# Moving one batch's gates, factors and projections ahead of the others, with the other batches' projections between its first queries and scores

## The chip, the cores and the metric

The kernel runs on one core of one Trainium2 chip. The core has a matrix engine (TensorE, PE in the rows), a vector engine (VectorE, DVE), an activation engine (ScalarE, ACT), a general engine (GpSimd, POOL) and a queue engine for transfers (SyncE, SP). Each works through its own list of instructions in order; semaphores join the lists. The time is that of one execution on the device, in microseconds.

## What is computed

One decoder layer over x of 4 batches x 512 tokens x 256 features: a layernorm, attention with 16 heads of 128, a layernorm and a residual; then a layernorm, a mixture of 8 experts (2 chosen for each token) plus a shared network, a layernorm and a residual. The attention is the part that matters here:

```python
q = (x @ Wq.T).reshape(b, n, H, D)
kv = x @ Wkv.T
kv_head = x @ Wkvh.T
g = x @ Wg.T
log_f = jnp.concatenate([jnp.zeros((b, 1, 2 * H), jnp.float32), jax.nn.log_sigmoid(g)], axis=1)
log_f_cumsum = jnp.cumsum(log_f, axis=1)[:, :-1]
kv_head = kv_head * jnp.exp(log_f_cumsum)
kv_head = jnp.cumsum(kv_head, axis=1)
kp, vp = (kv[..., :D], kv[..., D:])
kh, vh = (kv_head[..., :H], kv_head[..., H:])
k = jnp.einsum('bnd,bnh->bnhd', kp, kh)
v = jnp.einsum('bnd,bnh->bnhd', vp, vh)
q = rope(q)
k = rope(k)
```

Keys and values are shared by all heads but for a factor for each head and token. That factor is a running sum of a projection, weighted by a running product of sigmoids (the gates). Scores are masked to the past, a softmax and the weighing of values follow, and a projection out.

## The kernel before, in words

The order of the work is written out by hand, one list for each engine. A unit is one head of one batch; there are 64, batch by batch. Matrix products that must be as exact as float32 are made of three passes over operands that are split into a high and a low part (`three_pass`, L377): ACT or POOL rounds the high part, DVE or POOL subtracts to get the low one. Transposes (L765, L855) and the weighing of values (L869) are plain float32.

The front works on all four batches before the first unit. For each batch, DVE takes the statistics of x (L1102, L1105), ACT the root (L514), DVE the reciprocal and the normalized x (L1109, L1116). PE turns it (`turn_x`, L765), ACT and DVE split it (`head_of`, `rest_of`: xt_hi L521, xt_lo L1123). PE then projects gates, keys and values from w0, which POOL has split (w_hi L1530, w_lo L1532; the rows drop the number in a name). Keys are swapped on ACT (L534, L535), multiplied by cosines on DVE (L1130) and by sines on POOL (L1545), and summed on DVE into kt (L1136). When the gates of all batches are copied, ACT takes one sigmoid over 128 rows (L569) and DVE computes the factors of all batches at once (`factors`: scan L1146, product L1148, scan L1149). SP stores them in DRAM and loads each unit's key factors back as a row spread over 128 partitions (kh_row). PE turns them into columns (L931) that scale the turned probabilities (vcol, L647).

Queries of a unit (L377) are swapped on ACT (L577, L578), rotated on DVE and POOL (L1176, L1560, L1565), and split by ACT (q_hi L611) and POOL (q_lo L1569). Keys of a unit are scaled on POOL (L1574) and split by ACT (k_hi L605) and DVE (k_lo L1203). Then follow scores on PE (L837), maxima on DVE (L1184), exponentials on ACT (L589), turned probabilities on PE (L855), whose eviction scales them (ACT L598, DVE L1197), weighing of values (L869), division by the sums (DVE L1211), a split of the output (ACT L617, POOL L1579) and its projection (L885). Queries run four units ahead, scores two. In units 1 to 8, DVE also takes the rest of a later head's wq (`rest_of_wq`, L1223), in units 1 to 14 the rest of a head's wo (L1228).

## Time and profile before

| what | us |
|---|---|
| runs of the kernel | 839.72, 846.82, 848.85 (median 846.82) |
| the profiled execution | 842.17 |
| its span in the trace | 840.40 |
| what lies around the span | 1.77 |
| busy: PE, DVE, POOL, ACT | 760.9, 614.5, 553.7, 490.4 |

The span is what the trace covers. The rows give, for an instruction, its start from the span's start and its length; an engine's idle time before it and what ended that stand in brackets.

### The profile page before, as it was taken

Reading aid. Unit: us, or ns where it says so; the run is one execution under the profiler, and the core shown is the slowest. Engines: PE = TensorE matmul, PEld = TensorE weight load, DVE = VectorE, ACT = ScalarE, POOL = GpSimd, SP = SyncE. Lnnn points to the kernel's source line nnn. Section 1 sums busy time; section 2 is a strip of 40 time slices with the busy share of each in tenths; the row PEclk is TensorE's granted clock in tenths of the full one; section 3 lists DMA queues with packets and bytes.
Section 4 is the critical chain, followed back from the end, with each engine's and each line's share of the span. In section 5 each row is a group of like instructions: output and inputs, shape, how many; then the busy total and the mean of one; then the engine's idle time right before and its main releaser. Section 6 shows DMA issues by size and latency. Waiting matters only on the chain.

```text
...
## 1 busy us (share of the span) xinstructions
PE 760.9 (91%) x4344; PEld 634.0 (75%) x4344; DVE 614.5 (73%) x1561; ACT 490.4 (58%) x1155; POOL 553.7 (66%) x460
## 2 busy tenths in 40 slices
...
GB/s 305 50 88 58 69 83 151 136 136 64 64 76 62 66 70 63 72 64 64 77 64 64 76 63 64 72 43 26 128 82 72 110 144 186 186 76 94 100 88 51
DMA packets 47701, 75.74 MB, mean 90 GB/s; under 512 B 9680, under 2 KB 24592, under 8 KB 47632
## 3 DMA queue, kind: packets, MB, share of 16 engines
...
q8 instruction: 34, 0.56, 0.3%
q14 instruction: 35, 0.29, 0.1%
...
## 4 chain that ended last, share of the span: by engine, by line
PE 75%; DVE 9%; ACT 5%; issue 5%; another core or an unknown queue 3%; POOL 2%; DMA 1%; DVEq 0%; ACTq 0%; POOLq 0%
PE ps L377 19%; PE ps L869 17%; PE ps L837 14%; PE ps L885 11%; PE ps L855 8%; PE ps L980 5%; DVE xn L1116 1%; DVE hid_both L1468 1%; DMA x_sb<-in_x_dram 1%; DVE hid_hi L1458 1%; DVE hid L1463 1%; DVE hid L1455 1%; DVE s_hid L1396 1%; ACT y_sb L750 1%
## 5 line engine op out<-in xcount | busy, mean ns | idle before, releaser
L589 ACT ACTIVATE prob<-ps,neg_max 128x512 f32<-128x512 f32 (+3 forms) x256 | 132.6, 526 | 86.2 <-DVE neg_max L1184 86.2
L869 PE MATMUL ps<-pt,vp 128*128 128x512 f32 (+3 forms) x512 | 150.7, 437 | 4.6 <-issue 3.1
L869 PEld LDWEIGHTS ps<-pt,vp 128*128 128x128 f32 x512 | 83.2, 192 | 54.6 <-issue 19.1
L1569 POOL TENSOR_TENSOR q_lo<-q_sw,q_hi 128x512 fp32r<-128x512 f32 x64 | 85.9, 1342 | 47.9 <-ACT q_hi L611 47.9
L1184 DVE CUSTOM_DVE_ANT_0 ps<-ps,causal_row 128x512 f32<-128x512 f32 (+3 forms) x256 | 117.4, 520 | 0.0
L1579 POOL TENSOR_TENSOR o_lo<-o_t,o_hi 128x512 fp32r<-128x512 f32 x64 | 83.3, 1301 | 47.3 <-ACT o_hi L617 46.8
L837 PE MATMUL ps<-k_hi,q_hi 128*128 128x512 f32 (+3 forms) x256 | 91.0, 355 | 7.3 <-POOL q_lo L1569 5.0
L855 PE MATMUL ps<-id_f,prob 128*128 128x128 f32 x640 | 92.3, 275 | 2.4 <-ACT pt L598 2.4
L1203 DVE TENSOR_TENSOR k_lo<-kh_row,k_hi 128x512 fp32r<-128x512 f32 x64 | 83.4, 1303 | 8.1 <-ACT k_hi L605 8.1
L1560 POOL TENSOR_TENSOR q_sw<-q_sw,rope_sb 128x512 f32<-128x512 f32 x64 | 83.7, 1307 | 8.7 <-ACT q_sw L578 8.7
L1565 POOL TENSOR_TENSOR q_sw<-q_cos,q_sw 128x512 f32<-128x512 f32 x64 | 81.5, 1274 | 9.2
L1574 POOL TENSOR_TENSOR kh_row<-kt,kh_row 128x512 f32<-128x512 f32 x64 | 85.5, 1336 | 0.0
L1197 DVE TENSOR_SCALAR pt<-ps,vcol 128x384 f32<-128x384 f32 (+2 forms) x192 | 82.1, 476 | 2.9 <-PE ps L855 2.8
L837 PE MATMUL ps<-k_hi,q_lo 128*128 128x512 f32 (+3 forms) x256 | 83.9, 328 | 0.0
L837 PE MATMUL ps<-k_lo,q_hi 128*128 128x512 f32 (+3 forms) x256 | 83.8, 327 | 0.0
L1176 DVE TENSOR_TENSOR q_cos<-ps,rope_sb 128x512 f32<-128x512 f32 x64 | 44.2, 690 | 53.0 <-ACT q_sw L578 52.7
L855 PEld LDWEIGHTS ps<-id_f,prob 128*128 128x128 f32 x640 | 72.5, 140 | 11.2 <-issue 2.9
L980 PE MATMUL ps<-sdn_sb,s_hid 128*128 128x256 f32 (+1 forms) x192 | 55.8, 437 | 19.0 <-DVEq L1376 16.2
L577 ACT COPY q_sw<-ps 64x512 f32<-64x512 f32 x64 | 37.3, 582 | 51.4 <-PE ps L377 48.9
L980 PEld LDWEIGHTS ps<-sdn_sb,s_hid 128*128 128x128 f32 (+1 forms) x192 | 37.5, 210 | 35.8 <-ACT y_sb L691 16.8
L1396 DVE TENSOR_TENSOR s_hid<-s_sg,ps 128x512 f32<-128x512 f32 (+1 forms) x24 | 16.1, 686 | 63.8 <-PE ps L377 22.6
L377 PE MATMUL ps<-xt_hi,wq_hi 128*128 128x512 f32 x128 | 52.7, 412 | 7.1 <-DVE q_cos L1130 6.2
...
## 6 DMA issues: line engine op xcount, KB each, us to landing
kh_row<-kvh_rows SPq DMA_DIRECT2D x64, 256.0 KB, 3.2
inv_row<-inverse_sums SPq DMA_DIRECT2D x64, 256.0 KB, 3.1
...
```

The costliest lines, as they stand in the source:

```text
L377: last = pe.matmul(psum, w(o), m(o), start=(o == 0 and j == 0), stop=(o == EO - 1 and j == 2))
L589: ins = act.activation(prob[:, i % 2, ROW_AT[nt]:ROW_AT[nt] + w], ps_s[bank][:, at:at + w], ACT.Exp, scale=-1.0, bias=neg_max[:, i % 2, nt ...
L837: ins = pe.matmul(ps_s[bank][:, at:at + w], q_[:, r, qs], k_[:, r, 0:w], start=(nt == tiles[0] and j == 0), stop=(nt == tiles[-1] and j == 2))
L855: ins = pe.transpose(ps_pt[bank][:, dst:dst + P], prob[:, i % 2, src:src + P], id_f[:])
L869: ins = pe.matmul(ps_qo[:, mt * P:SEQ], vp[:, b * TPB + mt, :], pt[:, i % 2, cols], start=(mt == 0), stop=(mt == PT_BANKS[-1][-1]))
L885: ins = pe.matmul(ps_acc[t // 2][:, at:at + E], o_[:, r, t * P:(t + 1) * P], w[:, h, :], start=(h == 0 and j == 0 and t % 2 == 0), stop=(h ...
L980: ins = pe.matmul(ps[6 + half][:, q * E:(q + 1) * E], s_hid[0:SHW[n][i], j % 2, i, t * P:(t + 1) * P], sdn_sb[0:SHW[n][i], n, i, :], start ...
L1184: ins = dve.tensor_tensor_reduce(s_, s_, causal_row[:, (NT - 1 - nt) * P:], 1.0, BIG, ALU.add, ALU.min, neg_max[:, i % 2, nt:nt + 1])
L1203: dve.tensor_tensor(k_lo[:, i % 2, :], kh_row[:, i % 2, :], k_hi[:, i % 2, :].bitcast(F32), ALU.subtract) \
L1560: pool.tensor_tensor(q_sw[:], q_sw[:], sin_sb, ALU.mult).then_inc(q_sin_ready, 1)
L1569: pool.tensor_tensor(q_lo[:, i % 2, :], q_sw[:], q_hi[:, i % 2, :].bitcast(F32), ALU.subtract) \
L1574: pool.tensor_tensor(kh_row[:, i % 2, :], kt[:, tok(batch(i))], kh_row[:, i % 2, :], ALU.mult) \
```

## The change

Batch 0 goes first and alone through gates, factors and projections, so that its factors can be stored while the others' projections have yet to be made. Those of batches 1 to 3 stand on PE between the first queries and scores. The factors are computed twice: for batch 0 (32 rows) in the front, and for all batches (128 rows) on DVE in units 0 to 3, stored in unit 4, turned on PE in unit 5. The sigmoid is now an exponential on ACT and an add and a reciprocal on DVE. Units 0 and 1 use plain float32 queries and keys (`PLAIN = 2`), with no split; their keys are scaled on DVE. Keys of a batch are summed on POOL instead of DVE. The root, the reciprocal and the normalizing of x for batches 1 to 3 go to POOL and ACT. The split of w0 goes to ACT and, after x of batch 0 is normalized, POOL. The rest of wq for heads 8 to 15 goes from DVE to POOL, in units 1 to 8. x of batch 0 is loaded in two halves, from two queues; the cosines and sines come after it. The diff, cut to its core:

```diff
+        FACTOR_STEP = 5
...
+        PLAIN = 2
+        q_rot = place("q_rot", Y_AT + 8 * KB, [PLAIN, SEQ])
+        kh = place("kh", Y_AT + 12 * KB, [PLAIN, SEQ])
...
-            sp.dma_start(x_sb[:, 0:TPB, :], x_v[0]).then_inc(x_in[0], 16)
+            sp.dma_start(x_sb[:, 0:2, :], x_v[0, :, 0:2, :]).then_inc(x_in[0], 16)
+            sp.dma_start(w0_raw[:], w0).then_inc(w0_in, 16)
             sp.dma_start(id_f[:], ident).then_inc(id_in, 16)
-            sp.dma_start(w0_raw[:], w0).then_inc(w0_in, 16)
...
-            sp.dma_start(kvh_dram, hc_t).then_inc(kvh_stored, 16)
+            sp.dma_start(kvh_dram[0:2 * H, :], hc_t[0:2 * H, :]).then_inc(kvh_stored, 16)
...
-            load_shared(0)
...
+                if i == FACTOR_STEP - 1:
+                    sp.wait_ge(hc_ready, 2)
+                    sp.dma_start(kvh_dram[2 * H:, :], hc_t[2 * H:, :]).then_inc(kvh_stored, 16)
+                if i == FACTOR_STEP:
+                    sp.wait_ge(kvh_stored, 32)
+                    load_shared(0)
...
+            act.dma_start(x_sb[:, 2:TPB, :], x_v[0, :, 2:TPB, :]).then_inc(x_in_rest, 16)
...
+                act.activation(f_t[rows, :], src[2 * H:4 * H, :], ACT.Exp, scale=-1.0).then_inc(gate_copied, 1)
...
+                if i == FACTOR_STEP:
+                    factors_as_columns(1)
                 if wq_head(i) is not None:
...
+            def turn_factors(k):
+                pe.wait_ge(hc_ready, k + 1)
+                bank, n = (5, 2 * H * B) if k else (3, 2 * H)
+                for mt in range(TPB):
+                    ins = pe.transpose(ps[bank][:, mt * n:(mt + 1) * n], hc_t[0:n, mt * P:(mt + 1) * P], id_f[0:n, 0:n])
+                ins.then_inc(vcol_psum, 1)
...
-                        for j, (q_, k_) in enumerate(((q_hi, k_hi), (q_hi, k_lo), (q_lo, k_hi))):
+                        passes = ((q_rot, kh),) if i < PLAIN else ((q_hi, k_hi), (q_hi, k_lo), (q_lo, k_hi))
+                        for j, (q_, k_) in enumerate(passes):
...
+            turn_x(0)
+            gates(0)
+            keys(0)
+            values(0)
+            turn_x(1)
             queries(0)
+            gates(1)
+            keys(1)
+            values(1)
             queries(1)
+            turn_x(2)
+            turn_factors(0)
+            pe.wait_ge(k_cos_ready, 1)
             pe.wait_ge(vcol_ready, 1)
             scores(0)
             queries(2)
+            gates(2)
+            keys(2)
+            values(2)
+            turn_x(3)
             scores(1)
+            gates(3)
+            keys(3)
             queries(3)
+            values(3)
             pe.wait_ge(v_ready, B)
             for i in range(UNITS):
...
                 weigh_values(i)
+                if i == FACTOR_STEP:
+                    turn_factors(1)
...
+            def sigmoids(k):
+                n = 2 * H * B if k else 2 * H
+                dve.wait_ge(gate_copied, B if k else 1)
+                done(dve.tensor_scalar(f_t[0:n, :], f_t[0:n, :], 1.0, None, ALU.add))
+                done(dve.reciprocal(f_t[0:n, :], f_t[0:n, :]))
...
-                if i and wq_head(i - 1) is not None:
-                    rest_of_wq(wq_head(i - 1))
+                if i == 0:
+                    sigmoids(1)
+                if i == 1:
+                    products_of_gates(1)
+                if i == 2:
+                    scaled_gates(1)
+                if i == 3:
+                    sums_of_gates(1)
...
             pool.wait_ge(w0_hi_ready, 1)
+            pool.wait_ge(xn_ready, TPB)
             pool.tensor_tensor(w0_lo[:], w0_raw[:], w0_hi[:].bitcast(F32), ALU.subtract).then_inc(w0_split, 1)
...
                 if i + 3 < UNITS:
                     rest_of_queries(i + 3)
+                if i and wq_head(i - 1) is not None:
+                    rest_of_wq(wq_head(i - 1), wq_head(i - 1) + 1)
```

On DVE in the front, before the change, the factors of all batches (128 rows) stand behind the keys of three batches:

```order
L1130 SCALAR_TENSOR_TENSOR q_cos<-ps,rope_sb 128x512 [waits k_swapped,kt_ready]
L1123 TENSOR_TENSOR xt_lo<-ps,xt_hi 128x512 [waits xt_hi_ready] x2
L1136 TENSOR_TENSOR kt<-q_cos,q_sw 128x512 [waits k_sin_ready,k_cos_ready]
L1130 SCALAR_TENSOR_TENSOR q_cos<-ps,rope_sb 128x512 [waits k_swapped,kt_ready]
L1136 TENSOR_TENSOR kt<-q_cos,q_sw 128x512 [waits k_sin_ready,k_cos_ready]
L1144 MEMSET fcum_t 128x1
L1146 SCALAR_TENSOR_TENSOR fcum_t<-f_t,ones_t 128x511 [waits f_ready]
L1148 TENSOR_TENSOR kvh_t<-kvh_t,fcum_t 128x512 [waits dve_c]
L1149 SCALAR_TENSOR_TENSOR hc_t<-ones_t,kvh_t 128x512 [waits dve_c]
L1130 SCALAR_TENSOR_TENSOR q_cos<-ps,rope_sb 128x512 [waits k_swapped,kt_ready]
L1136 TENSOR_TENSOR kt<-q_cos,q_sw 128x512 [waits k_sin_ready,k_cos_ready]
```

After it, batch 0's factors (32 rows: add, reciprocal, scan, product, scan; a scan is listed as SCALAR_TENSOR_TENSOR) stand ahead of the rest of x of batch 1 (xt_lo):

```order
L1185 TENSOR_SCALAR f_t<-f_t 32x512 [waits gate_copied]
L1186 RECIPROCAL f_t<-f_t 32x512 [waits dve_c]
L1190 MEMSET fcum_t 32x1 [waits dve_c]
L1191 SCALAR_TENSOR_TENSOR fcum_t<-f_t,ones_t 32x511
L1177 SCALAR_TENSOR_TENSOR k_cos<-ps,rope_sb 128x512 [waits k_swapped,rope_in,dve_c]
L1196 TENSOR_TENSOR kvh_t<-ps,fcum_t 32x512
L1203 SCALAR_TENSOR_TENSOR hc_t<-ones_t,kvh_t 32x512 [waits dve_c]
L1170 TENSOR_TENSOR xt_lo<-ps,xt_hi 128x512 [waits xt_hi_ready] x2
L1207 TENSOR_TENSOR q_cos<-ps,rope_sb 128x512 [waits q_swapped]
```

The factors moved from behind the keys to a place ahead of the second batch's split, and two instructions of a new kind joined them.

On ACT ahead of the first unit, before the change, the second unit's exponentials (L589) follow the third unit's query swap and splits, and a copy of values (vp) is long past:

```order
L577 COPY q_sw<-ps 64x512 [waits q_ready,q_psum]
L578 COPY q_sw<-ps 64x512
L605 CAST k_hi<-kh_row 128x512 [waits s_psum,kh_scaled]
L611 CAST q_hi<-q_sw 128x512 [waits s_psum,q_sum_ready]
L589 ACTIVATE prob,row_sum<-ps,neg_max 128x512 [waits max_ready]
L589 ACTIVATE prob,row_sum<-ps,neg_max 128x384 [waits max_ready]
L589 ACTIVATE prob,row_sum<-ps,neg_max 128x128
L589 ACTIVATE prob,row_sum<-ps,neg_max 128x256 [waits max_ready]
L548 CAST wo_hi<-wo_raw 128x256 [waits wo_in0] x2
```

After it, the gates, keys and values of the last batch (kvh_t, f_t, k_sw, vp) stand directly ahead of them:

```order
L552 COPY kvh_t<-ps 32x512 [waits gate_psum]
L553 ACTIVATE f_t<-ps 32x512
L560 ACTIVATE k_sw<-ps 64x512 [waits kt_ready,k_psum]
L561 ACTIVATE k_sw<-ps 64x512
L565 COPY vp<-ps 128x512 [waits v_psum]
L592 ACTIVATE prob,row_sum<-ps,neg_max 128x512 [waits max_ready]
L592 ACTIVATE prob,row_sum<-ps,neg_max 128x384 [waits max_ready]
L592 ACTIVATE prob,row_sum<-ps,neg_max 128x128
L592 ACTIVATE prob,row_sum<-ps,neg_max 128x256 [waits max_ready]
L574 CAST wo_hi<-wo_raw 128x256 [waits wo_in0] x2
```

The exponentials of the second unit now wait for the last batch's values on PE.

On DVE at the start of unit 0, before the change, from the rest of wo to the eviction of turned probabilities (pt):

```order
L1228 TENSOR_TENSOR wo_lo<-wo_raw,wo_hi 128x256 [waits wo_hi_ready,vcol_ready]
L1228 TENSOR_TENSOR wo_lo<-wo_raw,wo_hi 128x256 [waits wo_hi_ready]
L1217 RECIPROCAL row_inv<-row_sum 128x4 [waits exp_ready]
L1218 STREAM_TRANSPOSE inv_t<-row_inv 128x128 [waits dve_c]
L1176 TENSOR_TENSOR q_cos<-ps,rope_sb 128x512 [waits q_swapped]
L1197 TENSOR_SCALAR pt<-ps,vcol 128x384 [waits pt_psum]
L1197 TENSOR_SCALAR pt<-ps,vcol 128x128
L1197 TENSOR_SCALAR pt<-ps,vcol 128x256 [waits pt_psum]
```

After it:

```order
L1254 TENSOR_TENSOR wo_lo<-wo_raw,wo_hi 128x256 [waits wo_hi_ready,vcol_ready]
L1254 TENSOR_TENSOR wo_lo<-wo_raw,wo_hi 128x256 [waits wo_hi_ready]
L1248 RECIPROCAL row_inv<-row_sum 128x4 [waits exp_ready]
L1249 STREAM_TRANSPOSE inv_t<-row_inv 128x128 [waits dve_c]
L1185 TENSOR_SCALAR f_t<-f_t 128x512 [waits gate_copied]
L1186 RECIPROCAL f_t<-f_t 128x512 [waits dve_c]
L1207 TENSOR_TENSOR q_cos<-ps,rope_sb 128x512 [waits q_swapped,dve_c]
L1228 TENSOR_SCALAR pt<-ps,vcol 128x384 [waits pt_psum]
L1228 TENSOR_SCALAR pt<-ps,vcol 128x128
L1228 TENSOR_SCALAR pt<-ps,vcol 128x256 [waits pt_psum]
```

An add and a reciprocal over 128 rows and 512 columns came between the inverses of the sums and the cosine.

## Rows read from the trace of the kernel before

**Rows 1.** Engine busy time in stretches: us, busy us (x instructions) by engine, clock, DMA, GB/s

```profile
42.00:62.00 20.00, 11.97 (x54) 10.34 (x55) 7.13 (x8) 6.41 (x11) 9.49 (x8) 0.70 0.29 92
...
80.90:150.40 69.50, 66.04 (x382) 54.45 (x383) 69.23 (x146) 49.50 (x127) 53.25 (x41) 1.00 0.31 99
```

**Rows 2.** The chain that ended last, its start: start us, us, what

```profile
0.73 5.26 DMA x_sb<-in_x_dram
...
8.49 3.16 DVE xn L1116 x4
...
15.21 2.91 PE ps L377 x6
...
21.36 1.38 DVE xn L1116 x4
...
28.40 1.09 PE ps L765 x8
...
29.50 6.81 PE ps L377 x42
...
49.47 0.58 ACT q_sw L577
```

**Rows 3.** Timeline of the front: start us, us, engine, line, instruction, idle before it

```profile
8.14 0.82 POOL L1530 CAST w_hi<-w_raw 128x768 fp32r<-128x768 f32 x1 [7.09 <-DMA w_raw<-in_w_dram]
...
38.84 2.38 POOL L1537 TENSOR_TENSOR wq_lo<-wq_raw,wq_hi 128x1024 fp32r<-128x1024 f32 x1
...
38.99 2.79 DVE L1136 TENSOR_TENSOR kt<-q_cos,q_sw 128x512 f32<-128x512 f32 x1 [0.67 <-POOL q_sw L1545]
...
41.70 1.21 DVE L1146 TENSOR_TENSOR_SCAN fcum_t<-f_t,ones_t 128x511 f32<-128x511 f32 x1
...
42.95 0.69 DVE L1148 TENSOR_TENSOR kvh_t<-kvh_t,fcum_t 128x512 f32<-128x512 f32 x1
...
57.83 0.77 PE L837 MATMUL ps<-k_hi,q_hi 128*128 128x512 f32 x1 [3.50 <-POOL q_lo L1569]
...
77.12 1.26 DVE L1197 TENSOR_SCALAR pt<-ps,vcol 128x384 f32<-128x384 f32 x3
```

**Rows 4.** DMA issues of the first 80 us: count, KB each, median us to landing

```profile
rope_sb<-in_cos_t_dram ACTq DMA_DIRECT2D x1, 256.0 KB, 4.4
```

**Rows 5.** Groups of DVE instructions by shape: busy us, mean ns

```profile
L1217 DVE RECIPROCAL row_inv<-row_sum 128x4 f32<-128x4 f32 x64 | 10.8, 169 | 4.2 <-ACT prob L589 4.2
...
L1435 DVE RECIPROCAL cw<-den 128x16 f32<-128x16 f32 x1 | 0.3, 253 | 0.0
```

**Rows 6.** Stretches of the front, as in rows 1; the clock follows PEclk's place after POOL

```profile
9.00:11.70 2.70, 0.00 (x0) 0.00 (x0) 2.70 (x5) 0.00 (x0) 1.80 (x1) 1.00 1.11 349
...
46.50:49.90 3.40, 3.37 (x10) 2.71 (x11) 0.66 (x1) 0.43 (x1) 0.00 (x0) 0.50 0.32 120
...
57.80:63.60 5.80, 5.77 (x17) 5.05 (x18) 0.69 (x1) 1.74 (x4) 3.78 (x3) 0.50 0.08 25
```

**Rows 7.** Timeline of one unit between 99.6 and 108.4 us

```profile
99.75 1.29 POOL L1579 TENSOR_TENSOR o_lo<-o_t,o_hi 128x512 fp32r<-128x512 f32 x1 [0.60 <-ACT o_hi L617]
...
100.06 1.25 DVE L1223 TENSOR_TENSOR wq_lo<-wq_raw,wq_hi 128x256 fp32r<-128x256 f32 x1
...
101.00 1.46 POOL L1574 TENSOR_TENSOR kh_row<-kt,kh_row 128x512 f32<-128x512 f32 x1
...
103.45 2.40 PE L869 MATMUL ps<-pt,vp 128*128 128x512 f32 x8 [0.41 <-issue]
...
105.22 0.69 ACT L589 ACTIVATE prob<-ps,neg_max 128x512 f32<-128x512 f32 x1 [1.80 <-DVE neg_max L1184]
```

**Rows 8.** Page, costliest groups: busy us, mean ns, idle before

```profile
L589 ACT ACTIVATE prob<-ps,neg_max 128x512 f32<-128x512 f32 (+3 forms) x256 | 132.6, 526 | 86.2 <-DVE neg_max L1184 86.2
```

**Rows 9.** Timeline of POOL in units 10 and 11

```profile
166.13 1.79 POOL L1569 TENSOR_TENSOR q_lo<-q_sw,q_hi 128x512 fp32r<-128x512 f32 x1 [0.73 <-ACT q_hi L611]
...
174.08 1.79 POOL L1569 TENSOR_TENSOR q_lo<-q_sw,q_hi 128x512 fp32r<-128x512 f32 x1 [0.73 <-ACT q_hi L611]
```

More of the change, by code:

```diff
@@ L235, in decoder_layer @@
         neg_half = small("neg_half", [TPB])
+        neg_mean = small("neg_mean", [TILES])
         neg_max, row_sum = (small(n, [2, NT]) for n in ("neg_max", "row_sum"))
@@ L847, in turn_probs @@
                         pe.wait_ge(pt_rest_ready, 2 * i - 1)
+                    if k == 1 and i == FACTOR_STEP + 1:
+                        pe.wait_ge(vcol_ready, 2)
                     if k == 2:
@@ new lines, in scaled_gates, with sums_of_gates @@
+            def scaled_gates(k):
+                n = 2 * H * B if k else 2 * H
+                done(dve.tensor_tensor(kvh_t[0:n, :], kvh_t[0:n, :] if k else ps[GATE_BANK[0]][0:n, :], fcum_t[0:n, :], ALU.mult))
+            def sums_of_gates(k):
+                n = 2 * H * B if k else 2 * H
+                if k:
+                    dve.wait_ge(vcol_ready, 1)
+                    dve.wait_ge(kvh_stored, 16)
+                dve.tensor_tensor_scan(hc_t[0:n, :], ones_t[0:n, :], kvh_t[0:n, :], 0.0, ALU.mult, ALU.add).then_inc(hc_ready, 1)
```

349 lines of the change are left out of this document (175 added, 174 removed).

## Prediction

> **What bounds the kernel now.** I read the time by stage first [rows 1]. From 80.9 to 150.4 us, which is eight of the 64 attention units (1 to 8), VectorE (DVE) is busy 69.23 of 69.50 us: it sets a pace of 8.7 us a unit, and TensorE (PE) follows. From 42 to 62 us PE is busy 11.97 of 20 us and no engine more than that: a stretch of waits. So the change, which rearranges what lies ahead of the first units, can gain there, and whatever it hands DVE or POOL in units 0 to 8 costs time.
>
> The chain that ended last then shows what the front is made of [rows 2]. x of batch 0 takes 5.26 us to land; normalizing it takes DVE 3.16 us where the same four instructions take 1.38 us for batch 2; the first projection starts at 15.21. The 42 matmuls from 29.50 on (gates, values, gates, keys) take 6.81 us. The timeline of the late front [rows 3] has the gates' scan at 41.70, PE idle for 3.50 us before the first scores at 57.83, and at 77.12 DVE's first eviction of turned probabilities, my **marker**: from there on DVE has no rest.
>
> The same rows show a rule for DVE and POOL. At 38.99 DVE's sum of two SBUF tiles takes 2.79 us: it ends 0.56 us after POOL's 2.38 us split that began at 38.84. One waits until the other is through. The slow 3.16 us of [rows 2] lie beside POOL's split of w0, which begins at 8.14.
>
> **The change, part by part.** I follow the clock of the profiled execution (842.17 us, span 840.40) to the marker, then count the units.
>
> *To the first gates.* x of batch 0 now comes as two halves of 256 KB, first on two queues. The nearest row is the cosine table, 256 KB and first on ACT's queue, issued at 0.74: 4.4 us, so 5.14 [rows 4] instead of 5.99: 0.85 us gained. The split of w0 now waits until x is normalized: 3.16 becomes 1.38, 1.78 us gained. Against that, x of batch 1 is 1216 KB deep in SP's queue and DVE reads its statistics before the rest of batch 0. w0, 960 KB deep in the old order, was there at 8.14 [rows 3]; 256 KB more at 349 GB/s [rows 6] make 0.7 us alone and twice that if ACT's queue takes its share, so 8.9 to 9.6, where DVE would be free at 9.0. I take 0.6 us lost, bounds 0 and 1. The first gates start at 15.21 - 0.85 - 1.78 + 0.6 = 13.2.
>
> *The gates' factors.* Six matmuls at the low clock take 2.91 us [rows 2], the exponential on ACT 0.6 as its other 512-column copies (the one at 49.47): 16.7. Then DVE works in order: add one, reciprocal over 512 columns, scan, cosine of the keys, product, second scan, and only then the rest of x of batch 1, for which the second gates wait. Add, cosine, product and each of the two rests I take at 0.69 us, as the product at 42.95, and a scan at 1.21 [rows 3]. The reciprocal is the unknown. Its rows [rows 5] give 169 ns for 4 columns and 253 ns for 16: 7 ns a column, so 0.169 + 508 x 0.007 = 3.7 us. If the slope is an accident of small tiles, it is as long as another 512-column instruction, 0.6 us. I take 3.7, since a slope between rows of the same instruction is the nearest evidence, and keep 0.6 for the range.
>
> With 0.6 us for the second scan's wait behind POOL's sum of the keys, DVE takes 0.6 + 3.7 + 1.2 + 0.7 + 0.7 + 0.6 + 1.2 + 1.4 = 10.1 us: the second gates start at 26.8. PE has nothing to do from about 23: its keys, values and first queries are 36 matmuls, 5.8 us by the rate of [rows 2], with the turn of batch 1 7 us behind the first gates' end at 16.1.
>
> *To the first scores.* Gates, keys and values of batch 1 and one head's queries are the same 42 matmuls: 6.81 us. After idle stretches of 6.1 and 3.5 us, PE ran at a granted clock of 0.50 (1.2 of 2.4 GHz) for 3.4 and 5.8 us [rows 6]; after an idle 3.8 us I add 2.5 us. The turn of batch 2 (1.09 at the high clock [rows 2]) stands before the first scores on PE, and on ACT its heads stand before the swap of the second queries and the copy of the factors: 0.6 + 1.2 + 0.4 us. The factors' bank holds the first scores back: 26.8 + 6.8 + 2.5 + 1.1 + 2.2 = 39.4, against 57.83 [rows 3].
>
> *To the marker.* That head start of 18 us is not kept. Between the first scores and unit 0 now lie the blocks of batches 2 and 3 with two queries (2 x 6.81), a turn (1.09) and two scores. A plain score has the shapes of a unit's weighing of values, 2.40 us [rows 7], and I charge that; what plain scores take away are the splits of keys and queries on ACT, POOL and DVE, which no longer stand in this path. Together 19.5 us: values of batch 3 end at 58.9. The second unit's exponentials now stand behind the copy of these values on ACT. So: copy 0.6, exponentials 4 x 0.526 [rows 8], two splits of wo 0.8, DVE's rest of wo 0.4, inverses 0.5, then the new add and second reciprocal 0.6 + 3.7, 0.1 between them, and the cosine 0.7: 9.5 us. The marker falls at 68.4 instead of 77.12: **8.7 us gained**.
>
> *Units 1 to 3.* DVE's rest of wq goes, scans and a product come. In before's unit the rest of wq is 1.25 us long, but until 101.04 it waits for POOL's o_lo, so only 0.27 of it is work [rows 7]; a scan of 1.21 in its place ends 0.94 later, POOL's kh_row waits behind it and DVE's rest of wo behind that. About 1.0 each for the two scans, 0.4 for the product. POOL's new rest of wq costs some 0.75 us (2.38 for 1024 columns and 1.29 for 512, carried on to 256) ahead of o_lo in units 2 and 3: 0.3 each. Lost: 3.0 us; bounds 0 and 5.
>
> *Units 4 to 8.* DVE is relieved, but POOL is not free: in a later unit, 7.95 us from q_lo to q_lo, its only idle time is the 0.73 us in which it waits for q_hi [rows 9]. With 0.75 more it comes to 8.7, what DVE needed before; 0.5 of q_lo's 1.79 is a wait for DVE that may go. Gained 0 to 2.5, I take 0.5.
>
> *Unit 5.* The factors of the other batches are turned on PE after that unit's weighing, and ACT stops for them before its exponentials. In before's unit the weighing ends at 105.85, the exponentials start at 105.22 [rows 7]; with the turn, the copy and a split of wq they start some 2 us later, and q_hi, q_lo and the next scores with them. Lost: 2.0; bounds 0.5 and 2.5.
>
> Later loads, the deferred load of the shared weights and everything from unit 9 on are alike. **Sum:** -8.7 + 3.0 - 0.5 + 2.0 = -4.2 us, 842.17 becomes 838.0. The median of the runs, 846.82, lies 4.65 above the profiled execution; I forecast it at 838.0 + 4.6 = 842.6. About 1% is what a measurement of this kernel can tell from no change.
>
> **The rivals.** *The reciprocal is as fast as other instructions.* Then the front and unit 0 each lose 3.1 us: 842.6 - 6.2 = 836.4, faster by 1.2%. For it: only two short tiles show the slope. Against: it is the same instruction and 84 ns for twelve columns are no noise.
>
> *The units swallow the new work.* POOL's gaps and the vanished wait of q_lo hide the rest of wq, ACT catches up after unit 5: the 5.0 us of units 1 to 5 fall away, 837.6. For it: ACT is busy 49.50 of 69.50 us there and POOL 53.25 [rows 1]. Against: DVE is full, and its waits are chained to POOL's.
>
> *PE stays at the low clock.* From 39.4 to 58.9 PE has queries, blocks, turns and scores with a wait before many of them; if two thirds of this run at 0.50, as did 57.8 to 63.6 [rows 6], the 19.5 us grow by 13: 855.6, slower. It decides from some 4 us of it on. Against: 6.81 us for 42 matmuls at 29.50 came in a stretch as dense as this one.
>
> **How the numbers follow.** Forecast 0.52; fast reciprocal 0.16 and swallowed work 0.20, together faster by over 1% with 0.36; low clock 0.12, slower by over 1%; within 1% 0.52. The range, 831 to 853, goes from the fast reciprocal with all of the swallowed work (836.4 - 5.0) to the forecast with eight of the low clock's 13 us and the upper bounds of units 1 to 5 (2.5 more). The forecast's own range is 838.5 to 849.
>
> **What would show it.** Right: the first gates near 13 us, a reciprocal of 32x512 near 3.7, PE idle some 4 us before the second gates, the first scores near 39, the second unit's exponentials directly behind the last copy of values, the marker near 68, unit 1 above 9 us, a gap before the exponentials of unit 7. Wrong: a marker before 65 or after 72, units 1 to 3 at 8.7 us or less, or units 4 to 8 at 8.0.

## The result, and the profile after

| | before | changed | changed, measured again |
|---|---|---|---|
| median of the runs, us | 843.35 (12 runs) | 833.94 (12 runs) | 835.23 (4 runs; before beside it: 842.98) |
| ratio to before, 95% interval | | 0.9876, 0.9857 to 0.9895 | 0.9899, 0.9884 to 0.9914 |
| span of the profiled execution | 840.40 | 833.2 | 834.1 |
| first gates | 15.21 | 13.49 | 13.81 |
| second gates | | 27.19 | 27.51 |
| first scores | 57.83 | 37.35 | 39.14 |
| marker: first eviction of turned probabilities | 77.12 | 64.90 | 66.67 |
| turned row sums of unit 12 | 167.67 | 156.59 | 158.32 |
| from there to the end of the span | 672.7 | 676.6 | 675.8 |

The change makes the kernel faster by 1.0 to 1.2%, 8 to 10 us. That is inside the range (831 to 853), but below the forecast's own range (838.5 to 849): faster by over 1%, which had 0.36, came, and not the likeliest case. Of the 8.7 us between the forecast (842.6) and the median, 3.5 are the starting point, since the three runs of the kernel before that it stood on have a median of 846.82 and all twelve one of 843.35. The other 5.2 are the change: 4.2 us forecast, 9.4 measured. The last row of the table is scatter: over the fourteen profiled executions of this study, which all run the same work there, it lies between 672.2 and 676.6. The two executions of the changed kernel happen to have its highest values; from unit 12 to unit 63 they are within 0.5 us of the kernel before, and the difference lies behind that. So I compare executions at unit 12, and below that by the length of a stage.

The timeline of the changed kernel's first profiled execution (start us, us, engine, line, instruction, idle before it), in the order in which the prediction walked:

```profile
6.68 1.38 DVE L1163 TENSOR_SCALAR xn<-x_sb,mv,rstd 128x256 f32<-128x256 f32 x4
...
8.22 1.81 POOL L1586 TENSOR_TENSOR w_lo<-w_raw,w_hi 128x768 fp32r<-128x768 f32 x1 [7.17 <-DVE xn L1163]
...
10.06 1.40 DVE L1148 BATCH_NORM_STATS2 stats<-x_sb 128x6 f32<-128x256 f32 x4 [2.00 <-DMA x_sb<-in_x_dram]
...
12.07 1.28 DVE L1170 TENSOR_TENSOR xt_lo<-ps,xt_hi 128x512 fp32r<-128x512 f32 x2
...
13.49 0.77 PE L387 MATMUL ps<-xt_hi,w_hi 128*128 128x512 f32 x1 [3.34 <-DVE xt_lo L1170]
...
18.06 3.34 DVE L1186 RECIPROCAL f_t<-f_t 32x512 f32<-32x512 f32 x1
...
27.19 0.47 PE L387 MATMUL ps<-xt_hi,w_hi 128*128 128x512 f32 x1 [3.39 <-DVE xt_lo L1170]
...
37.35 2.40 PE L861 MATMUL ps<-kh,q_rot 128*128 128x512 f32 x8 [1.84 <-issue]
39.40 0.59 PE L387 MATMUL ps<-xt_hi,wq_hi 128*128 128x512 f32 x1
...
56.82 0.69 ACT L592 ACTIVATE prob<-ps,neg_max 128x512 f32<-128x512 f32 x1
...
59.37 0.76 DVE L1254 TENSOR_TENSOR wo_lo<-wo_raw,wo_hi 128x256 fp32r<-128x256 f32 x2 [5.03 <-ACT wo_hi L574]
...
60.91 3.35 DVE L1186 RECIPROCAL f_t<-f_t 128x512 f32<-128x512 f32 x1
...
64.90 1.26 DVE L1228 TENSOR_SCALAR pt<-ps,vcol 128x384 f32<-128x384 f32 x3
...
65.09 4.61 PE L896 MATMUL ps<-pt,vp 128*128 128x512 f32 x8 [2.69 <-issue]
```

They answer to [rows 2, 3]. Normalizing takes 1.38 us instead of 3.16, since POOL's split starts behind it. VectorE then waits 2.00 us for x of batch 1, and the rest of x of batch 0 stands behind those statistics. The reciprocal takes 3.34 us; TensorE waits 3.39 us for what VectorE does after it. First scores start 20.5 us earlier than before, the marker 12.2. The last rows are unit 0: VectorE idles 5.03 us, then runs a second reciprocal of 3.35 us for which everything waits, and TensorE, idle for 2.69 us, weighs at half speed (4.61 us; 2.40 in [rows 7]).

Stretches of the same execution, as in [rows 1] (us, busy us by engine, granted clock after POOL's column): unit 0's weighing, and units 1 to 8.

```profile
65.00:69.80 4.80, 4.61 (x8) 2.28 (x8) 3.04 (x12) 2.67 (x9) 2.53 (x2) 0.50 0.00 0
...
71.15:140.26 69.11, 66.89 (x394) 55.61 (x393) 57.53 (x140) 50.30 (x128) 60.28 (x48) 1.00 0.39 115
```

The granted clock of the weighing is 0.50, 1.2 of 2.4 GHz. VectorE, 69.23 of 69.50 us busy before, is now busy 57.53 of 69.11, and POOL 60.28 instead of 53.25. Units 1 to 9 last 9.55, 8.54, 9.03, 8.12, 9.46, 8.04, 8.35, 8.02, 8.35 us (from one turned row sums to the next), where before's first eight lasted 8.72 each and the ninth 7.58.

### The profile page after: what moved, and what is told of

The parts are those of the page before. It is cut to its first block, busy times and chain, and to the rows that moved or that the text cites. A ratio compares the mean times of both kernels' runs of the same rounds, so it can differ in the third digit from the quotient of the medians.

```text
span 833.2 us, 13978 instructions
## 1 busy us (share of the span) xinstructions
PE 756.6 (91%) x4340; PEld 629.5 (76%) x4340; DVE 598.4 (72%) x1548; ACT 492.8 (59%) x1159; POOL 562.6 (68%) x473
## 4 chain that ended last, share of the span: by engine, by line
PE 72%; DVE 7%; POOL 6%; issue 5%; ACT 5%; another core or an unknown queue 3%; DMA 1%; SPq 0%; DVEq 0%; ACTq 0%; POOLq 0%
PE ps L387 21%; PE ps L896 15%; PE ps L861 12%; PE ps L912 9%; PE ps L882 7%; PE ps L1023 6%; POOL o_lo L1643 1%; POOL q_lo L1633 1%; POOL kh_row L1638 1%; DMA x_sb<-in_x_dram 1%; POOL q_sw L1629 1%; POOL q_sw L1621 1%; DVE hid_both L1523 1%; ACT prob L592 1%
## 5 line engine op out<-in xcount | busy, mean ns | idle before, releaser
L1643 POOL TENSOR_TENSOR o_lo<-o_t,o_hi 128x512 fp32r<-128x512 f32 x64 | 85.2, 1332 | 43.3 <-ACT o_hi L620 43.3
L1633 POOL TENSOR_TENSOR q_lo<-q_sw,q_hi 128x512 fp32r<-128x512 f32 x62 | 83.5, 1347 | 42.3 <-ACT q_hi L614 42.3
L861 PE MATMUL ps<-k_hi,q_hi 128*128 128x512 f32 x248 | 87.1, 351 | 0.0
L1629 POOL TENSOR_TENSOR q_sw<-q_cos,q_sw 128x512 f32<-128x512 f32 x62 | 78.9, 1272 | 11.7 <-DVE q_cos L1207 2.9
L1638 POOL TENSOR_TENSOR kh_row<-kt,kh_row 128x512 f32<-128x512 f32 x62 | 83.5, 1346 | 0.0
L861 PE MATMUL ps<-k_lo,q_hi 128*128 128x512 f32 x248 | 80.3, 324 | 0.0
L861 PE MATMUL ps<-k_hi,q_lo 128*128 128x512 f32 x248 | 80.1, 323 | 0.0
L1207 DVE TENSOR_TENSOR q_cos<-ps,rope_sb 128x512 f32<-128x512 f32 x64 | 44.1, 688 | 49.6 <-ACT q_sw L581 49.2
L1234 DVE TENSOR_TENSOR k_lo<-kh_row,k_hi 128x512 fp32r<-128x512 f32 x62 | 74.1, 1196 | 0.0
L1242 DVE TENSOR_TENSOR o_t<-ps,inv_row 128x512 f32<-128x512 f32 x64 | 44.2, 691 | 15.1 <-PE ps L896 14.3
```

The lines of the kernel that those rows point to most:

```text
L861: ins = pe.matmul(ps_s[bank][:, at:at + w], q_[:, r, qs], k_[:, r, 0:w], start=(nt == tiles[0] and j == 0), stop=(nt == tiles[-1] and j == ...
L1629: pool.tensor_tensor(q_sw[:], q_cos[:], q_sw[:], ALU.add).then_inc(q_sum_ready, 1)
L1633: pool.tensor_tensor(q_lo[:, i % 2, :], q_sw[:], q_hi[:, i % 2, :].bitcast(F32), ALU.subtract) \
L1638: pool.tensor_tensor(kh_row[:, i % 2, :], kt[:, tok(batch(i))], kh_row[:, i % 2, :], ALU.mult) \
L1643: pool.tensor_tensor(o_lo[:, i % 2, :], o_t[:], o_hi[:, i % 2, :].bitcast(F32), ALU.subtract) \
```

## The experiments

Times and starts, for all of them (the ratio is to the kernel before, run beside each):

| run | median | ratio (95%) | first scores | marker | unit 12 |
|---|---|---|---|---|---|
| second reciprocal earlier | 829.49 | 0.9831 (0.9794 to 0.9868) | 40.07 | 64.12 | 154.75 |
| sigmoid of batch 0 on ScalarE | 831.54 | 0.9856 (0.9818 to 0.9893) | 34.42 | 61.96 | 154.30 |
| factors copied late | 832.69 | 0.9860 (0.9824 to 0.9896) | 40.28 | 69.50 | 160.11 |
| rest of wq back on VectorE | 839.00 | 0.9945 (0.9923 to 0.9967) | 40.03 | 67.58 | 164.51 |
| rest of x first | 832.15 | 0.9877 (0.9853 to 0.9901) | 38.29 | 65.84 | 157.46 |
| before, rest of wq on POOL | 839.74 | 0.9959 (0.9941 to 0.9977) | 59.17 | 78.48 | 165.30 |
| before, new loads | 841.25 | 0.9978 (0.9956 to 1.0001) | 56.92 | 76.23 | 166.81 |
| no plain units | 836.89 | 0.9929 (0.9905 to 0.9953) | 37.65 | 70.04 | 161.15 |
| the three combined | 824.18 | 0.9777 (0.9763 to 0.9790) | 35.26 | 60.98 | 150.57 |
| front in another order | 822.16 | 0.9743 (0.9728 to 0.9759) | 32.95 | 58.68 | 148.21 |
| split of w0 at once | 833.27 | 0.9885 (0.9869 to 0.9901) | 38.87 | 66.43 | 158.08 |

**The changed kernel again.** No edit.

> The changed kernel unaltered, a second profiled execution of it. Theory: TensorE's clock in the second gates differs from execution to execution, since three kernels with this same front showed 512-column matmuls of 0.77 us there and the first scores at 40.0 to 40.3 where the first profiled execution of the changed kernel had 0.47 and 37.35; so first scores at either 37.4 or 40.1, everything from unit 1 on in the same periods (9.55, 8.54, 9.03, 8.12, 9.46, 8.04, 8.35, 8.02). Rival, it is the edits that moved the clock: first scores at 37.4 again. Ratio 0.9876 by both.

Timeline and stretches of the second execution:

```profile
27.51 0.76 PE L387 MATMUL ps<-xt_hi,w_hi 128*128 128x512 f32 x1 [4.28 <-DVE xt_lo L1170]
...
39.14 2.40 PE L861 MATMUL ps<-kh,q_rot 128*128 128x512 f32 x8 [1.85 <-issue]
```

```profile
27.50:30.20 2.70, 2.69 (x6) 2.13 (x7) 2.40 (x11) 0.00 (x0) 1.44 (x2) 0.50 0.37 104
...
30.70:34.00 3.30, 3.30 (x26) 3.08 (x25) 0.67 (x2) 2.10 (x4) 3.13 (x8) 1.00 0.07 27
```

The clock differs, without any edit: 0.50 from 27.5 to 30.2 here, 1.00 in the first execution. From second gates to first scores it is 11.63 us, there 10.16. The three kernels that the expectation means (second reciprocal earlier, factors copied late, rest of wq back on VectorE) show 12.69, 12.99 and 12.71. So a front in which TensorE waits some 3 to 5 us (2.9 to 5.1) before the second gates came out with the low clock in six of eight executions and without it in two. That is part of why single runs differ by 3 us. The Trainium skill (TensorE: Matmul & The Clock Gate, What's actually happening) says that how many matmuls of one kernel run cold, at the low clock, differs from run to run; these traces agree, with 0 and 1.5 us in two executions of one kernel and 2.5 in others with the same front. The periods of units 1 to 8 are the same to 0.03 us.

**Second reciprocal earlier.**

```diff
             cos_of_keys(3)
+            sigmoids(1)
             dve.wait_ge(vcol_ready, 1)
...
-                if i == 0:
-                    sigmoids(1)
```

> The changed kernel with the add and the second reciprocal (128x512) taken out of unit 0 and put where VectorE waits 5.03 us for the head of wo, behind the cosine of batch 3's keys. Theory A, the chain ahead of the units goes 1:1 to the end: the marker (first eviction of turned probabilities) falls from 64.90 to 61.1, the turned row sums of unit 12 from 156.6 to 152.8, and to 150.5 if the weighing of unit 0 also runs at the high clock then (2.32 instead of 4.61 us); the median near 830, ratio to the kernel before 0.981 to 0.984. Theory B, the units' own pace decides and swallows a head start: the marker at 61.1 too, but unit 12 within 1 us of 156.6 and the ratio at 0.987.

The timeline of this kernel, VectorE and TensorE ahead of unit 0:

```profile
57.94 3.35 DVE L1186 RECIPROCAL f_t<-f_t 128x512 f32<-128x512 f32 x1
...
62.11 0.76 DVE L1254 TENSOR_TENSOR wo_lo<-wo_raw,wo_hi 128x256 fp32r<-128x256 f32 x2 [0.82 <-ACT wo_hi L574]
...
64.94 2.32 PE L896 MATMUL ps<-pt,vp 128*128 128x512 f32 x8
```

The reciprocal sits in the idle time, of which 0.82 us are left, and the weighing runs in 2.32 us. This execution had the slower second gates, so it is read from the first scores: 24.05 us to the marker instead of 27.55, and 114.68 to unit 12 instead of 119.24, 4.6 us less: 3.5 ahead of the marker, and 1.1 behind it, where the half-speed weighing stood. The median fell by 4.5 against 833.94, though the intervals of the two ratios overlap. Theory A holds, and the half-speed weighing was part of the reciprocal's price.

**Sigmoid of batch 0 on ScalarE.**

```diff
-                act.activation(f_t[rows, :], src[2 * H:4 * H, :], ACT.Exp, scale=-1.0).then_inc(gate_copied, 1)
+                if b:
+                    act.activation(f_t[rows, :], src[2 * H:4 * H, :], ACT.Exp, scale=-1.0).then_inc(gate_copied, 1)
+                else:
+                    act.activation(f_t[rows, :], src[2 * H:4 * H, :], ACT.Sigmoid).then_inc(gate_copied, 1)
+                    act.activation(std[:, 8:9], eps_sb[:, 0:1], ACT.Exp)
```

VectorE's add and reciprocal stay for the other batches (k = 1).

> The changed kernel with the sigmoid of batch 0 on ScalarE, as the kernel before has it, in place of exponential, add and first reciprocal (32x512); one small exponential behind it brings ScalarE's exponential table back. Theory A, VectorE's chain of the factors sets the front: 3.75 us fewer on it, the second gates start at 23.9 instead of 27.19 with nothing left of TensorE's 3.39 us of idle, first scores at 34 instead of 37.35, marker at 61.6, ratio 0.984. Rival: the transfers set it (the factors' way through DRAM and back, 27.53 to 32.1, or x of batch 2), then the second gates come at 24 but the first scores stay within 1 us of 37.35 and the ratio at 0.987.

The timeline of this kernel from ScalarE's sigmoid to the first scores:

```profile
15.69 1.28 ACT L556 ACT_TABLE_LOAD   x1
...
17.59 1.28 ACT L557 ACT_TABLE_LOAD   x1
...
17.61 1.21 DVE L1196 TENSOR_TENSOR_SCAN fcum_t<-f_t,ones_t 32x511 f32<-32x511 f32 x1 [1.63 <-issue]
...
24.28 0.47 PE L387 MATMUL ps<-xt_hi,w_hi 128*128 128x512 f32 x1 [1.23 <-DVE xt_lo L1174]
...
34.42 2.40 PE L865 MATMUL ps<-kh,q_rot 128*128 128x512 f32 x8 [1.85 <-issue]
```

The scan starts at 17.61, where the add stood. Both table loads (1.28 us each) are there, the second while ScalarE has nothing else to do. Second gates and first scores come 2.9 us earlier than in the first execution of the changed kernel, and TensorE stays at the high clock: theory A, but for 1.23 us of TensorE's wait that are left where it had none. Of the 2.9 us, 2.3 are left at unit 12, since unit 1 takes 10.15 us instead of 9.55; the median is 2.4 us lower.

**Factors copied late.**

```diff
-                if i == FACTOR_STEP:
-                    factors_as_columns(1)
                 if wq_head(i) is not None:
...
                     exps(i + 2, [1, 2])
+                if i == FACTOR_STEP:
+                    factors_as_columns(1)
```

> The changed kernel with the copy of the other batches' factors put behind unit 7's exponentials on ScalarE (in its list for unit 5), where it stood ahead of them. Theory: ScalarE's 2.10 us of waiting for the turned factors is what makes unit 5 take 9.46 us beside 8.0 to 8.4 of its neighbours: unit 5 falls to 8.2, unit 12 from 156.6 to 155.4, ratio 0.9860. Rival: TensorE's four turns and the wait in front of unit 6's second bank make the unit long, or the copy then holds the head of the output: unit 5 and 6 together stay within 0.3 us of 17.5, ratio 0.9876.

ScalarE's copy in the timeline of the changed kernel:

```profile
112.41 0.32 ACT L652 COPY vcol<-ps 128x192 f32<-128x192 f32 x1 [2.10 <-PE ps L832]
```

The same copy in this kernel, and the exponential it now follows:

```profile
118.36 0.47 ACT L592 ACTIVATE prob<-ps,neg_max 128x256 f32<-128x256 f32 x1
...
118.81 0.32 ACT L652 COPY vcol<-ps 128x192 f32<-128x192 f32 x1
```

The 2.10 us of waiting are gone; unit 5 takes 8.22 us instead of 9.46, unit 6 8.22 instead of 8.04. Marker to unit 12 is 90.61 instead of 91.69: 1.1 us, as the theory has it. The ratios alone would not tell it (the intervals overlap).

**Rest of wq back on VectorE, and before with it on POOL.** The same edit in both directions; in the kernel before:

```diff
-                if i and wq_head(i - 1) is not None:
-                    rest_of_wq(wq_head(i - 1))
...
                     rest_of_queries(i + 3)
+                if i and wq_head(i - 1) is not None:
+                    rest_of_wq(wq_head(i - 1), wq_head(i - 1) + 1)
```

The first of these two kernels takes POOL's lines out of the changed kernel's unit and gives VectorE its `rest_of_wq` back, ahead of the rest of wo.

> The changed kernel with the rest of wq for heads 8 to 15 back on VectorE, as before the change. By the prediction's terms: units 1 to 3 lose about 1 us each (VectorE has the rest of wq and the scans), units 4 to 8 go from 8.0 to 8.4 back to 8.7: unit 12 at 160 to 162, ratio 0.992 to 0.994. Rival, what POOL is rid of makes up for it: unit 12 within 1 us of 156.6, ratio 0.987 to 0.989.

> The kernel before with one part of the change alone: the rest of wq for heads 8 to 15 goes from VectorE to the end of POOL's unit. Theory A, the rest of wq is what holds VectorE at 8.72 us a unit: units 1 to 8 take 8.0 to 8.4, unit 9 some 0.8 longer, so the turned row sums of unit 12 come 2.5 to 4 us earlier than 167.67, counted from the marker, and the ratio is 0.995 to 0.997. Theory B, it is the way in which VectorE and POOL wait for each other (a rest of wq is 0.38 us of work and 1.25 with its wait): the unit stays at 8.5 to 8.8 with the wait elsewhere, ratio 0.999 to 1.002.

With it back on VectorE, units 1 to 8 take 10.18, 10.42, 10.84, 8.95, 9.95, 8.12, 8.13, 8.13: marker to unit 12 is 96.93 instead of 91.69, 5.2 us more, and the median 5.1 more. The sum is as expected (unit 12 at 161.8, if counted from the first scores of the changed kernel's first execution; the ratio is just above its range), its place is not: units 1 to 5 lose 5.6 us, up to 1.9 each, and units 6 to 8 take 8.1 us where 8.7 was expected. With it on POOL in the kernel before, units 1 to 8 take 65.25 us instead of 69.74 and unit 9 0.75 more: 3.7 us less from marker to unit 12, and a ratio of 0.9959. These are theory A's times, but the cause is theory B's. The timeline of VectorE and POOL in the kernel before, from the end of unit 6 into unit 7:

```profile
124.01 1.29 POOL L1569 TENSOR_TENSOR q_lo<-q_sw,q_hi 128x512 fp32r<-128x512 f32 x1 [1.29 <-ACT q_hi L611]
...
124.22 1.62 DVE L1203 TENSOR_TENSOR k_lo<-kh_row,k_hi 128x512 fp32r<-128x512 f32 x1
...
125.89 1.28 POOL L1579 TENSOR_TENSOR o_lo<-o_t,o_hi 128x512 fp32r<-128x512 f32 x1 [0.59 <-ACT o_hi L617]
...
126.21 1.25 DVE L1223 TENSOR_TENSOR wq_lo<-wq_raw,wq_hi 128x256 fp32r<-128x256 f32 x1
```

The same place in the kernel before with the rest of wq on POOL:

```profile
122.41 0.68 DVE L1203 TENSOR_TENSOR k_lo<-kh_row,k_hi 128x512 fp32r<-128x512 f32 x1
...
123.02 1.29 POOL L1567 TENSOR_TENSOR q_lo<-q_sw,q_hi 128x512 fp32r<-128x512 f32 x1 [0.73 <-ACT q_hi L611]
...
124.26 0.74 POOL L1535 TENSOR_TENSOR wq_lo<-wq_raw,wq_hi 128x256 fp32r<-128x256 f32 x1
...
124.35 0.18 DVE L1217 RECIPROCAL row_inv<-row_sum 128x4 f32<-128x4 f32 x1 [1.26 <-ACT prob L589]
...
124.95 1.29 POOL L1577 TENSOR_TENSOR o_lo<-o_t,o_hi 128x512 fp32r<-128x512 f32 x1
```

Before, VectorE's rest of the keys (k_lo) starts 0.2 us after POOL's q_lo and takes 1.62 us, then the rest of wq starts 0.3 us after POOL's o_lo and takes 1.25. Without the rest of wq, VectorE comes to k_lo before POOL comes to q_lo and does it in 0.68; it even waits 1.26 us for ScalarE. POOL has 0.74 us more to do and is not late, since its own waits for ScalarE (1.29 and 0.59 us above) shrink to 0.73 and nothing. The Trainium skill (SBUF — State Buffer, SBUF: two separate sides) calls this a lock held for a whole instruction, by whichever engine starts first; the first fence agrees with that, since k_lo and the rest of wq end 0.5 and 0.3 us behind the instruction of POOL that began before them. How much of the 1.25 us was work shows in the changed kernel with the rest of wq on VectorE, in a unit of 8.13 us, where VectorE comes first:

```profile
130.34 0.68 DVE L1234 TENSOR_TENSOR k_lo<-kh_row,k_hi 128x512 fp32r<-128x512 f32 x1
...
132.52 0.38 DVE L1254 TENSOR_TENSOR wq_lo<-wq_raw,wq_hi 128x256 fp32r<-128x256 f32 x1
...
132.62 1.43 POOL L1650 TENSOR_TENSOR o_lo<-o_t,o_hi 128x512 fp32r<-128x512 f32 x1 [0.44 <-ACT o_hi L620]
```

In units 6 to 8 of this kernel VectorE and POOL run the same instructions in the same order as in units 6 to 8 of the kernel before, in 8.13 us a unit instead of 8.72. So 8.72 us was not the amount of VectorE's work: it was one of two rhythms of the same work, the one in which VectorE comes second each time. Moving the rest of wq ended that rhythm; what else would end it was not tested.

**Before, with the new loads.** Loads as in the change, and in front of POOL's split of w0:

```diff
             pool.wait_ge(w0_in, 16)
+            pool.wait_ge(xn_ready, TPB)
             pool.tensor_copy(w0_hi[:], w0_raw[:]).then_inc(w0_hi_ready, 1)
```

> The kernel before with the change's order of loads and with POOL's split of w0 held back until x of batch 0 is normalized. By the prediction's terms the first gates come 0.9 + 1.8 - 0.6 = 2.1 us earlier, at 13.1 to 13.5 instead of 15.21. Theory A, the front is one chain: the first scores come as much earlier than 57.83, ratio 0.9975. Theory B, the later batches set the front (their x, VectorE's and POOL's work on the keys): the first scores move by under 0.5 us, ratio 1.000.

First gates at 13.34, 1.9 us earlier; first scores 0.9 earlier than in the kernel before, and 2.25 earlier than in the run with the rest of wq on POOL, which has the kernel before's front (15.59 and 59.17). From first gates to first scores it is 43.58 us in these two runs and 42.62 in the kernel before. The difference is VectorE's normalizing of x of batch 2: it takes 2.35 and 2.36 us in the two runs, in which POOL multiplies keys by sines during it, and 1.38 in the kernel before. So all of the gain at the first gates reaches the first scores, less what VectorE and POOL lose to each other on the way: theory A is likelier, and the interval of the ratio just includes 1.

**Split of w0 at once, and the rest of x first.**

```diff
             pool.wait_ge(w0_hi_ready, 1)
-            pool.wait_ge(xn_ready, TPB)
```

> The changed kernel with POOL's split of w0 no longer held back until x of batch 0 is normalized. By the prediction's step the four normalizing instructions take up to 3.16 us instead of 1.38 and the first gates come up to 1.8 us later, ratio up to 0.990. Theory from the trace: the first gates wait for x of batch 1, so the first gates come at most 0.5 us later than 13.5 and the ratio stays at 0.9876 to 0.9885.

The timeline of this kernel up to the first gates:

```profile
6.68 2.87 DVE L1163 TENSOR_SCALAR xn<-x_sb,mv,rstd 128x256 f32<-128x256 f32 x4
...
10.07 1.41 DVE L1148 BATCH_NORM_STATS2 stats<-x_sb 128x6 f32<-128x256 f32 x4 [0.52 <-DMA x_sb<-in_x_dram]
...
13.50 0.77 PE L387 MATMUL ps<-xt_hi,w_hi 128*128 128x512 f32 x1 [1.87 <-DVE xt_lo L1170]
```

Normalizing beside the split takes 2.87 us instead of 1.38, so the two engines do hinder each other, but the first gates still start at 13.50: VectorE only waits 0.52 us for x of batch 1 instead of 2.00.

```diff
             normalize_first()
-            stats_of_x(1)
             rest_of(0)
+            stats_of_x(1)
...
             head_of(0)
-            normalize_x(1)
             gates_of(0)
+            normalize_x(1)
```

> The changed kernel with VectorE's rest of x of batch 0 ahead of the statistics of batch 1, and ScalarE's exponential of batch 0's gates ahead of its normalizing of batch 1. Theory: the first gates wait not for the normalized x but for the landing of x of batch 1, behind whose statistics (10.06 to 12.07) the rest of x of batch 0 stands; freed of it the first gates start at 11.9 instead of 13.5, the second gates 1 to 1.5 us earlier, ratio 0.986. Rival, the statistics of batches 1 and 2 then fall between gates and factors and cost there what was won: first gates at 11.9, second gates within 0.5 us of 27.2 to 27.4.

The first gates come at 11.53, the second at 26.71 with TensorE idle for 5.14 us: the rival. The timeline of POOL and VectorE between the two shows VectorE's negated mean of batch 2, 0.17 us of work for batch 1, held for 2.01 us until POOL's rest of wq is through; so the reciprocal starts only 0.5 us earlier than in the changed kernel:

```profile
14.75 2.38 POOL L1591 TENSOR_TENSOR wq_lo<-wq_raw,wq_hi 128x1024 fp32r<-128x1024 f32 x1
...
15.15 2.01 DVE L1154 TENSOR_SCALAR neg_mean<-mv 128x4 f32<-128x4 f32 x1
...
17.58 3.34 DVE L1186 RECIPROCAL f_t<-f_t 32x512 f32<-32x512 f32 x1
```

**No plain units.** `PLAIN = 0`, with the splits of units 0 and 1 put into the lists of ScalarE, VectorE and POOL, and the space of the swapped keys moved.

> The changed kernel with queries and keys of units 0 and 1 split and multiplied in three passes, as all others (the swapped and the cosine keys lie in the space of the turned probabilities for it). By the prediction's term, where a plain score takes 2.40 us and the splits fall away: a score of three passes is 4.0 us, so 1.6 more for each of two, and keys and queries of unit 0 pass ScalarE, POOL and VectorE once more, 2 to 3 us in front of the first scores: first scores 2 to 3 us later, marker 4 to 6 later, ratio 0.992 to 0.995. Rival, TensorE has other work there and fills the wait: under 2 us in all, ratio 0.988 to 0.990.

The timeline of this kernel from the first scores to the second:

```profile
37.65 0.47 PE L865 MATMUL ps<-k_hi,q_hi 128*128 128x512 f32 x1 [1.84 <-ACT vcol L655]
...
39.64 0.39 PE L387 MATMUL ps<-xt_hi,wq_hi 128*128 128x512 f32 x1
...
42.65 0.62 ACT L614 CAST q_hi<-q_sw 128x512 fp32r<-128x512 f32 x1 [5.10 <-POOL q_sw L1633]
...
49.13 1.47 PE L804 MATMUL ps<-id_f,xn 128*128 128x128 f32 x8 [2.59 <-ACT f_t L553]
```

The first scores start at 37.65 with the second gates at 27.49, the same 10.16 us as in the first execution: they are held back by the factors' columns, not by the splits. The marker comes 32.39 us after the first scores instead of 27.55, unit 12 4.3 us later counted in the same way; the ratio is 0.9929 instead of 0.9876. The size is the expected one, but not for the expected reason. From the start of the first scores to that of the next queries it is 1.99 us here (37.65 to 39.64) and 2.05 with plain scores (37.35 to 39.40), so the 1.6 us for each score are not there. The splits cost time behind the first scores: ScalarE waits 5.10 us for POOL before it splits the queries of unit 1, comes late to the gates of batch 2, and TensorE waits 2.59 us for it and 0.78 us once more. From 49.6 to 53.4 TensorE's clock is 0.50, and the second scores take 3.4 us instead of 2.0. What plain units save in the changed kernel is work of ScalarE, POOL and VectorE, as the prediction has it, and no time of TensorE in the scores.

**The three combined, and the front in another order.** The second takes the combined kernel and reorders the lists of VectorE and POOL as below; on ScalarE batch 0's gates and the first swap of queries move ahead of the normalizing of batches 1 and 2, and the small exponential goes behind the swapped keys of batch 0:

```diff
             normalize_first()
-            stats_of_x(1)
             rest_of(0)
-            stats_of_x(2)
+            stats_of_x(1)
             sigmoids(0)
             products_of_gates(0)
+            scaled_gates(0)
+            sums_of_gates(0)
             dve.wait_ge(rope_in, 32)
             cos_of_keys(0)
-            scaled_gates(0)
-            sums_of_gates(0)
+            stats_of_x(2)
             rest_of(1)
...
+            rest_of_wq(0, WCH)
             inverse_std(1)
-            rest_of_wq(0, WCH)
-            inverse_std(2)
             pool.wait_ge(rope_in, 32)
             roped_keys(0)
+            inverse_std(2)
```

> The changed kernel with the edits of the first three experiments together (second reciprocal ahead of unit 0, sigmoid of batch 0 on ScalarE, copy of the factors late). If each saves on its own piece of one chain: 4.5 + 2.4 to 3.3 + 1.1 us, so 8.0 to 8.9 us less than the changed kernel, unit 12 at 148 to 149 from a start at the high clock, ratio 0.977 to 0.978. If they overlap (a shorter front only makes the wait for the last values longer), no more than the largest of them: ratio 0.982.

> As the combined one, and the front in another order: VectorE takes the rest of x of batch 0 ahead of the statistics of batch 1, both scans ahead of the cosine of the keys, and the statistics of batch 2 behind them; POOL takes the rest of the first heads' wq first; ScalarE takes batch 0's gates ahead of the normalizing of batch 1. If VectorE's order is what keeps TensorE waiting, the first gates start at 11.5 and the second gates at 22.2 without idle time in front (24.28 with the sigmoid alone), first scores at 32.2, 2.2 us less than the combined one, ratio 0.975. Rival, TensorE runs the front at the low clock for longer, or POOL and ScalarE come late with batches 1 and 2: no gain over the combined one.

The timeline of the reordered one at first gates, second gates and first scores:

```profile
11.85 0.77 PE L387 MATMUL ps<-xt_hi,w_hi 128*128 128x512 f32 x1 [1.49 <-DVE xt_lo L1174]
...
22.79 0.47 PE L387 MATMUL ps<-xt_hi,w_hi 128*128 128x512 f32 x1 [1.02 <-DVE xt_lo L1174]
...
32.95 4.08 PE L865 MATMUL ps<-kh,q_rot 128*128 128x512 f32 x8 [1.84 <-issue]
```

The combined kernel is 9.8 us below 833.94 by the medians, 8.3 by the ratios: the savings add. Unit 12 comes at 150.57 and not at 148 to 149, since TensorE falls to the low clock in the first scores (3.72 us instead of 2.40, 0.50 from 36.2 to 39.6), which costs 1.7 us up to the marker: 25.72 us instead of the 24.05 of the second reciprocal earlier. The reordered one has the same (4.08 us above). The reordered front gains 2.0 us more, with 1.02 us of TensorE's wait before the second gates left. At 0.9743 (0.9728 to 0.9759) it is faster than both kernels of this case.

## Why the prediction was right and where not

**First gates, right in size and wrong in its terms.** 13.2 forecast, 13.49 and 13.81 measured. The 1.78 us of normalizing are real, but the split at once shows that they gain nothing; x of batch 1, which I took for a loss of 0.6, sets the time: it costs 2.0 us (11.53 with the rest of x first). A gain too much and a loss too small about cancel.

**Factors, right.** Second gates at 26.8, measured 27.19. So near a hit is partly luck: VectorE's add starts at 17.6 and not at 16.7, since ScalarE normalizes x of batch 1 (2.08 us) and loads a table (1.28 us) ahead of the exponential, and from there to the second gates it is 9.6 us and not 10.1. The reciprocal is 3.34 us where I took 3.7 from the slope of [rows 5]; the rival of a fast reciprocal is refuted. The estimate of 4.3 us from the Trainium skill (VectorE: DVE Perf Modes, Walkthrough) lies 1 us above the row; the measurement decides.

**The low clock's 2.5 us, right for most executions.** 12.69 - 10.16 = 2.5 us where it came in full, 1.5 in the second execution of the changed kernel, none in the first. First scores at 39.4 forecast, 37.35 and 39.14 measured. The rival that TensorE stays low through the other batches' blocks did not come: from first scores to last values both executions of the changed kernel show 1.00, and four other kernels of this study 3 to 4 us at 0.50 (no plain units, factors copied late, the three combined, front in another order). The long stretch at 0.50 of the first execution, some 7 us, lies around unit 0's weighing.

**To the marker, 29.0 forecast, 27.5 measured.** Some 0.9 us of it lie behind the last values (9.5 forecast, 8.6 measured), 0.5 ahead of them. What I had not seen is that TensorE's wait for the second reciprocal would make unit 0's weighing, behind the marker, 2.3 us longer; taking the reciprocal away showed it.

**Units 1 to 9, the step that failed.** I lost 3.0 us in units 1 to 3, 2.0 in unit 5, and gained 0.5 in 4 to 8: 4.5 lost. From marker to unit 12 the kernel before takes 90.55 us, the changed one 91.69 and 91.65: 1.1 lost. Of that 1.0 is the end of unit 0 (from the marker to where unit 1 begins, at 71.15, 6.25 us instead of 5.26, and 5.27 with the second reciprocal earlier), so units 1 to 9 lose 0.1. Units 1 to 3 lose 0.95. Units 4, 6, 7 and 8 gain 2.35 and not 0.5; unit 5 is 0.74 longer than 8.72, 1.3 to 1.4 longer than its neighbours, of which the late copy gets back 1.1 net; unit 9 loses 0.77, which I had not counted. What was wrong is the sentence that POOL, with 0.75 us more, comes to 8.7: it comes to 8.0 to 8.4, since I built on q_lo's 1.79 us of [rows 9], of which up to 0.5 is waiting, and POOL's waits took up the rest. Under it lies another: I read VectorE's 69.23 busy us as work that sets a pace of 8.7 us, and part of it was waiting for POOL (k_lo 1.62 us for 0.68 of work, the rest of wq 1.25 for 0.38). This is the rival that the units swallow the new work: of its 5.0 us, units 1 to 3 and 5 still lose 1.7, and the kernel before with this one edit shows the shorter unit.

**The sum.** Marker 10.45 us earlier in the second execution (8.7 forecast), 1.1 lost behind it (4.5 forecast): 5.2 us more than my 4.2, and 9.4 is what the medians show. Of the signs that I had named, the long wait before the second gates, unit 1 above 9 us and the gap before the exponentials of unit 7 came as signs of being right. Of those of being wrong, the marker before 65 just came in the first execution (64.90; 66.67 in the second), units 4 and 6 to 8 at 8.0 to 8.4 came, and of units 1 to 3 one is below 8.7 (8.54).

**What each part is worth,** by the runs that took one away or did one alone: rest of wq on POOL 3.7 to 5.2 us, plain units 4.3 (in the order that the run without them gave the splits), loads about 1.9 (perhaps nothing). If they add, they make all of the gain, and the new order of the batches with its two reciprocals about breaks even; that is argued, since no run took the order alone.
